# A third token tile's attention in halves, and a later gate, in an adaptive-layernorm transformer block

## What is computed

```python
mod = (silu(c) @ wmod).reshape(4, 6, 1, -1)            # c (4, 1024), wmod (1024, 6144)
sa, ca, ga, sb, cb, gb = (mod[:, i] for i in range(6))
ga, gb = (2 * (g >= 0) - 1) * max(abs(g), 0.25)        # for g = ga and g = gb
h = layernorm(x) * (1 + ca) + sa                       # x (4, 512, 1024)
x = x + ga * (h @ (weight * block_mask).T)             # "attention": 1024 x 1024, mask of 32 x 32 blocks
h = layernorm(x) * (1 + cb) + sb
x = x + gb * ffn(h)                                    # NF4 codes, hidden size 2752, silu(h w1) * (h w2) @ w3
```

## Time and profile before

| | |
|---|---|
| median of 3 runs | 1569.68 us (1569.42 to 1570.12) |
| the profiled execution's own time | 1569.33 us |
| its span, first to last instruction | 1567.6 us |
| outside the span | 1.7 us |
| PE busy in the span | 1539.4 us, 98% |
| DVE busy | 1029.5 us, 66% |
| ACT busy | 989.6 us, 63% |

### The profile page before, as it was taken

The page is one execution under the profiler, slowest core; times in us unless marked ns, Lnnn a source line. Parts: engine busy times, 40 slices in busy tenths (PEclk is TensorE's granted clock), DMA queues, the critical chain, the costliest instruction groups (busy, mean ns, idle before and its releaser), DMA issues.

```text
span 1567.6 us, 19154 instructions
## 1 busy us (share of the span) xinstructions
PE 1539.4 (98%) x7200; PEld 1269.6 (81%) x7200; DVE 1029.5 (66%) x1486; ACT 989.6 (63%) x1290; POOL 5.5 (0%) x10
## 2 busy tenths in 40 slices
PE   5899999999999999999999999999999999999999
PEld 3688888888888888888888888888888888888887
DVE  5687786555555455547676666666875757956994
ACT  3475676998888888884898988785433432333220
POOL 0000000000000000000000000000000000000000
PEclk9999999999999999999999999999999999999999
DMA  9976423564555445532778787786777868947973
GB/s 368 372 258 228 134 81 138 177 200 166 186 169 187 153 162 180 178 128 97 257 228 252 207 250 208 207 254 171 260 292 272 332 204 302 343 160 268 397 279 122
DMA packets 170139, 345.97 MB, mean 221 GB/s; under 512 B 14752, under 2 KB 65344, under 8 KB 170048
## 3 DMA queue, kind: packets, MB, share of 16 engines
q1 hardware_dynamic: 170048, 344.76, 65.1%
HBM read 249.77 MB, written 94.93 MB: 220 GB/s over the span
## 4 chain that ended last, share of the span: by engine, by line
PE 96%; DMA 2%; DVE 0%; ACT 0%; SPq 0%; issue 0%
PE ps L1916 10%; PE ps L1915 10%; PE ps L1914 10%; PE ps L1988 9%; PE ps L1987 9%; PE ps L1989 9%; PE ps L1925 9%; PE ps L1927 9%; PE ps L1926 9%; PE ps L1832 4%; PE ps L1834 4%; PE ps L1833 4%; DMA wmod<-wmod 2%; PE ps L1789 2%; PE ps L1772 1%; DVE attn_w_lo L1368 0%
## 5 line engine op out<-in xcount | busy, mean ns | idle before, releaser
L861 ACT ACTIVATE w_raw<-w_raw 128x1024 f32<-128x1024 f32 x287 | 304.6, 1061 | 9.1
L1914 PE MATMUL ps<-ffn_in_hi,w_hi 128*128 128x512 f32 x688 | 268.6, 390 | 0.0
L1916 PE MATMUL ps<-ffn_in_hi,w_lo 128*128 128x512 f32 x688 | 267.8, 389 | 0.0
L1915 PE MATMUL ps<-ffn_in_lo,w_hi 128*128 128x512 f32 x688 | 267.7, 389 | 0.0
L1987 PE MATMUL ps<-t_hi,s_hi 128*128 128x512 f32 x616 | 239.6, 389 | 0.0
L1988 PE MATMUL ps<-t_lo,s_hi 128*128 128x512 f32 x616 | 239.6, 389 | 0.0
L1989 PE MATMUL ps<-t_hi,s_lo 128*128 128x512 f32 x616 | 239.6, 389 | 0.0
L1925 PE MATMUL ps<-x_m_hi,stream_hi 128*128 128x512 f32 x604 | 235.0, 389 | 0.0
L1926 PE MATMUL ps<-x_m_lo,stream_hi 128*128 128x512 f32 x604 | 235.0, 389 | 0.0
L1927 PE MATMUL ps<-x_m_hi,stream_lo 128*128 128x512 f32 x604 | 235.0, 389 | 0.0
L1114 ACT ACTIVATE s_hi<-s_raw 128x1408 fp32r<-128x1408 f32 x56 | 77.4, 1383 | 241.2 <-DVE s_raw L1624 192.6
(11 more groups left out here) (136 smaller groups left out, 2078.1 us busy)
## 6 DMA issues: line engine op xcount, KB each, us to landing
s_raw<-h_d SPq DMA_DIRECT2D x96, 704.0 KB, 5.6
stream_raw<-t_d SPq DMA_DIRECT2D x150, 256.0 KB, 3.4
t_d<-combined SPq DMA_DIRECT2D x106, 256.0 KB, 2.6
wmod<-wmod SPq DMA_DIRECT2D x12, 2048.0 KB, 15.3
t_raw<-w_d SPq DMA_DIRECT2D x88, 256.0 KB, 6.1
w_codes<-w12q SPq DMA_DIRECT2D x41, 512.0 KB, 5.3
h_d<-h_tile SPq DMA_DIRECT2D x44, 256.0 KB, 2.4
h_d<-up_c SPq DMA_DIRECT2D x44, 256.0 KB, 3.3
```

Of the source, the lines that this page charges most:

```text
L861: act.activation(RAWF[r], RAWF[r] if j else RQ[r][:], ACT.Prelu, bias=bias, scale=sign, alpha=slope).then_inc(line_ready, 1)
L1914: pe.matmul(acc, RH[r][:, k, :], HH[:, b, k, :], start=(k == 0), stop=False)
L1915: pe.matmul(acc, RH[r][:, k, :], HL[:, b, k, :], start=False, stop=False)
L1916: last = pe.matmul(acc, RL[r][:, k, :], HH[:, b, k, :], start=False, stop=(k == C - 1))
```

## The change

Tile 2 is treated like tiles 0 and 1: its modulation and attention are done by halves of d, in PSUM banks 6 and 7, and its operands lie in two new tiles over a weight piece (80 and 84 KB). The transpose banks stay 4 and 5; group 1's wmod product moves to bank 4, group 2's (the gate) to bank 0, behind tile 0's `set_aside`; groups 3 to 5 stay in bank 6, now behind tile 2's residual. x of tile 2 is loaded ahead of mask pieces 2 and 3, which get places of their own. Parts 4 and 5 (the gate) are multiplied after all of tile 2's attention and after `turn1(3)`. Parts 6 and 7 move from behind tile 2 to behind tile 4, parts 8 and 9 from behind tile 5 to behind tile 6, their loads to t = 2 of SP's loop; group 3's rows are copied at t = 5 and turned after tile 5. On DVE `ln1(3)`, `ln1(4)`, `low_part1(3)` and `ln1(5)` come ahead of the gate, and `low_part1(4)` behind it, ahead of tile 0's residual. On ACT `input1(4)` comes ahead of `root(1, 0)`.

```diff
-    MOD_BANK, TURN_BANK, MASK_BANK = (0, 6, 6, 6, 6, 6), {0: 3, 1: 7, 3: 6, 4: 6}, 7
+    MOD_BANK, TURN_BANK, MASK_BANK = (0, 4, 0, 6, 6, 6), {0: 3, 1: 4, 3: 6, 4: 6}, 7
+    BY_HALVES = 3
+    HALF_TURNS = [(0, 0), (1, 0), (0, 1), (0, 2), (1, 1), (1, 2)]
...
@@ SP @@
             load_weight(0)
+            load_x(2)
             load_mask(2)
...
             load_weight(3)
-            sp.wait_ge(mask_step, MASK_STEPS + 2)
-            load_x(2)
             load_x(3)
...
             load_ga(TPB)
-            load_wmod(8)
...
-                if t == 1:
+                if t == 2:
+                    load_wmod(8)
                     load_wmod(9)
@@ ACT @@
             weight_high(0)
+            root(0, 2)
             act.wait_ge(mod_read, 2)
             half_input1(0, 0)
             half_input1(0, 1)
+            norm1(2)
+            half_input1(0, 2)
             weight_high(2)
...
             half_input1(1, 1)
+            start1(3)
+            half_input1(1, 2)
+            start1(4)
+            input1(3)
+            start1(5)
+            input1(4)
+            root(1, 0)
+            for t in range(2, TILES):
...
-                if t in (2, 6):
-                    copy_rows(t // 4 + 3)
+                if t in (5, 7):
+                    copy_rows(t // 2 + 1)
@@ DVE @@
             read_mod(0)
+            ln1_sums(2)
             split_weight(0)
             half_low_part1(0, 0)
+            ln1_factors(2)
             sum_mask(2)
...
             mask_weight(2)
+            half_low_part1(0, 2)
             split_weight(2)
...
-            ln1(2)
             ln1(3)
             set_aside(0)
-            low_part1(2)
+            half_low_part1(1, 2)
+            ln1(4)
             set_aside(1)
+            low_part1(3)
+            ln1(5)
             gate(0)
-            ln1(4)
-            ln1(5)
-            low_part1(3)
+            low_part1(4)
             residual_sum(0)
             residual_norm(0)
             for t in range(2, TILES):
                 residual_sum(t - 1)
-                if t == 2:
-                    low_part1(4)
-                elif t == 4:
+                if t == 4:
                     low_part1(5)
...
-                if t in (5, 8):
-                    read_mod(t // 3 + 2)
+                if t in (6, 8):
+                    read_mod(t // 2)
@@ PE @@
-                    if m == 2:
-                        pe.wait_ge(rows_read, 2)
+                    if m == 1:
+                        pe.wait_ge(half_modulated1, half_at(0, 2))
+                    elif m == 2:
+                        pe.wait_ge(gated, 1)
                     elif m == 3:
-                        pe.wait_ge(gate_step, 2)
+                        pe.wait_ge(gated, 3)
...
             attend_first(1, 0, 0)
+            half_turn1(0, 2)
             sum_partitions(1)
             modulation(2)
+            attend_first(2, 0, 0)
             modulation(3)
             attend_first(0, 1, 0)
             turn_mod(1, 1)
             attend_first(1, 1, 0)
             half_turn1(1, 1)
+            attend_first(2, 1, 0)
             attend_first(0, 0, 1)
             attend_first(0, 1, 1)
+            half_turn1(1, 2)
             attend_first(1, 0, 1)
-            turn1(2)
             attend_first(1, 1, 1)
+            turn1(3)
+            attend_first(2, 0, 1)
+            attend_first(2, 1, 1)
             modulation(4)
             modulation(5)
-            for t in range(2, TILES):
+            for t in range(BY_HALVES, TILES):
...
-                if t in (4, 7):
-                    turn_mod(t // 3 + 2, t // 3 + 1)
-                for j in {2: (6, 7), 5: (8, 9), 8: (10, 11)}.get(t, ()):
+                if t in (5, 7):
+                    turn_mod(t // 2 + 1, t // 2)
+                for j in {4: (6, 7), 6: (8, 9), 8: (10, 11)}.get(t, ()):
                     modulation(j)
```

More of the change, by code:

```diff
@@ L93, in adaln_kernel @@
     WM = [at(f"wmod_{i}", [C // 2, D], F32, kb) for i, kb in enumerate((0, 16, 64))]
-    MP = [at(f"mask_piece_{i}", [C // 2, HALF], I32, kb) for i, kb in enumerate((96, 104, ST + 8, ST + 28))]
+    MP = [at(f"mask_piece_{i}", [C // 2, HALF], I32, kb) for i, kb in enumerate((96, 104, 112, 120))]
     WP = [at(f"weight_piece_{i}", [C // 2, HALF], F32, kb) for i, kb in enumerate((80, 88, 128, 144))]
@@ L102, in adaln_kernel @@
     AL = [at(f"attn_in_lo_{i}", [C, P], F32R, 152 + 4 * i) for i in range(2)]
+    A3 = [at(f"attn_in_third_{n}", [C, P], F32R, kb) for n, kb in (("hi", 80), ("lo", 84))]
     raw_kb = (168, 172, 160, 164)
@@ L277, in adaln_kernel, with half_turns, half_at, attn_bank @@
     out_made = sem("out_made")
-    MOD_BANK, TURN_BANK, MASK_BANK = (0, 6, 6, 6, 6, 6), {0: 3, 1: 7, 3: 6, 4: 6}, 7
+    MOD_BANK, TURN_BANK, MASK_BANK = (0, 4, 0, 6, 6, 6), {0: 3, 1: 4, 3: 6, 4: 6}, 7
+    TURN_FROM = {0: 0, 1: QUARTER, 3: 0, 4: 0}
+    BY_HALVES = 3
+    HALF_TURNS = [(0, 0), (1, 0), (0, 1), (0, 2), (1, 1), (1, 2)]
+    def half_turns(half, t):
+        return HALF_TURNS.index((half, t)) + 1
+    def half_at(half, t):
+        return BY_HALVES * half + t + 1
+    def attn_bank(t):
+        return 6 if t == 2 else 2 * (t % 2)
+    def hi_of(t):
+        return A3[0] if t == 2 else AH[t % 2]
+    def lo_of(t):
+        return A3[1] if t == 2 else AL[t % 2]
     LN_STEPS, GATE_STEPS = 9, 5
@@ L295, in whole @@
     def whole(t):
-        return t - 1
+        return t - BY_HALVES + 1
     def place2(e):
@@ L911, in half_input1 @@
             def half_input1(half, t):
-                e = 2 * half + t
                 cs = slice(HALF_C * half, HALF_C * (half + 1))
-                act.wait_ge(half_turned, 2 * t + half + 1)
+                act.wait_ge(half_turned, half_turns(half, t))
                 if t:
-                    act.wait_ge(half_low1, e)
+                    act.wait_ge(half_low1, half_at(half, t) - 1)
                 for c in range(HALF_C * half, HALF_C * (half + 1)):
@@ L921, in half_input1 @@
                 ins.then_inc(half_modulated1, 1)
-                act.wait_ge(half_modulated1, e + 1)
-                act.activation(AH[t][:, cs, :], HM[0][:, cs, :], ACT.Copy).then_inc(half_high1, 1)
+                act.wait_ge(half_modulated1, half_at(half, t))
+                if t == 2:
+                    act.wait_ge(w_lo, weight_at(0))
+                act.activation(hi_of(t)[:, cs, :], HM[0][:, cs, :], ACT.Copy).then_inc(half_high1, 1)
             def input1(t):
                 act.wait_ge(turned1, whole(t))
-                if t >= 3:
+                if t > BY_HALVES:
                     act.wait_ge(low1, whole(t - 1))
                 else:
-                    act.wait_ge(half_low1, 4)
+                    act.wait_ge(half_low1, 2 * BY_HALVES)
                 modulate(4, HM[0], MODS[0], batch_of(t), modulated1, whole(t))
-                act.wait_ge(attn_done, t - 1)
+                act.wait_ge(attn_done, 1 if t == 4 else t - 1)
                 act.activation(AH[t % 2][:], HM[0][:], ACT.Copy).then_inc(high1, 1)
@@ L988, in _ @@
             half_input1(1, 1)
[L989 to L1007, removed]
+            start1(3)
[6 more added lines that the diff above has]
+            for t in range(2, TILES):
+                both = t - 2 >= HALF_TILES
+                if both:
+                    input2(t - 2 - HALF_TILES)
+                elif t > 4 and t + 1 < TILES:
+                    input1(t + 1)
+                root(1, t - 1)
+                if both and t + 1 < TILES:
+                    input1(t + 1)
                 if t == 3:
@@ L1276, in half_low_part1 @@
                 cs = slice(HALF_C * half, HALF_C * (half + 1))
-                dve.wait_ge(half_high1, 2 * half + t + 1)
-                dve.tensor_tensor(AL[t][:, cs, :], HM[0][:, cs, :], AH[t][:, cs, :].bitcast(F32), ALU.subtract).then_inc(half_low1, 1)
+                dve.wait_ge(half_high1, half_at(half, t))
+                dve.tensor_tensor(lo_of(t)[:, cs, :], HM[0][:, cs, :], hi_of(t)[:, cs, :].bitcast(F32), ALU.subtract).then_inc(half_low1, 1)
             def low_part1(t):
@@ L1839, in attend_half @@
                     pe.wait_ge(low1, whole(t))
-                    pe.wait_ge(gated, t - 1)
+                    if t == 4:
+                        pe.wait_ge(gate_step, 1)
+                    else:
+                        pe.wait_ge(gated, t - 1)
                 last = attend_part(t, hb, range(C))
@@ L1846, in attend_first @@
                 pe.wait_ge(w_lo, weight_at(2 * hb + half))
-                pe.wait_ge(half_low1, 2 * half + t + 1)
+                pe.wait_ge(half_low1, half_at(half, t))
                 last = attend_part(t, hb, range(HALF_C * half, HALF_C * (half + 1)))
```

28 lines of the change are left out of this document (14 added, 14 removed).

## The result

| | before | after |
|---|---|---|
| median of 5 runs | 1569.47 us | 1586.03 us (1585.74 to 1586.85) |
| ratio | | 1.0104 (1.009 to 1.0117) |
| profiled execution: time, span | 1569.33, 1567.6 us | 1585.9, 1583.9 us |

The change made the kernel slower by 16.6 us; the forecast was +16.4, between 1574 and 1590.

The account below looks back on a forecast made before the run. PE, fully busy from 84.6 us, was taken to bound the kernel, so only delays to PE count. The profiled 1569.33 plus 14.8 (late `turn1(7)` and parts 8, 9) plus 1.6 (clock) gave 1585.7 us, range 1574 to 1590.

Parts of the forecast that it names:

- The start: Up to part 5: tile 2's halves fill PE's early gaps; part 5 ends at 80.2, PE 4.4 us ahead.
- the lead: PE's gain on the old order at the end of part 5: 4.4 us, +-1 from DVE's split.
- The gate's move: Gate behind parts 4 and 5 lands at 90.3; tile 2's residual 3.7 us late; PE waits 5.9 us for `norm1(6)`.
- The loads in a row: Parts 8 and 9 issued together delay tile 3's x2 store; tile 7's x lands at 130.7, DVE waits 9 us.
- The rows' place: ACT copies group 3's rows only behind `norm1(7)`, until 138.8; PE waits from 128, `turn1(7)` starts at 139.75.
- The clock: Lower clock behind PE's 10 us gap ahead of group 3's turn: +1.6 us (0 to 3.4).
- the first term: At `turn1(7)`: 11.2 us late, with parts 8 and 9 (3.6 us) still ahead, summing to +14.8 us.
- the store's landing: Tile 3's x2 store, issued at 113.0 behind parts 8 and 9, lands at 126.4 (bounds 116.3 and 127).
- the gain is gone: At tile 6's turn: PE's 4.4 us lead is lost to a 5.9 us wait; tile 5's attention starts near 115.9.

Follow-up runs that it names:

- b_gate: The kernel before, with only the load of the attention gate for tile 0 held until tile 2's attention is done: 1573.39 us, ratio 1.0021.
- a_xslot: The changed kernel, with x of tile 7 in a place of its own, loaded behind the gate: 1576.16 us, ratio 1.0034.
- b_loads: The kernel before, with only the loads of wmod parts 8 and 9 moved, both to t = 2 of SP's loop: 1581.8 us, ratio 1.0069.
- b_loads_xslot: The kernel before, with wmod parts 8 and 9 both loaded at t = 2 and x of tile 7 in its own place: 1569.85 us, ratio 1.0001.
- a_rows: The changed kernel, with ACT copying group 3's rows at t = 4 instead of t = 5: 1583.64 us, ratio 1.0085.
- a_warm: The changed kernel, with 48 identity matmuls put into PE's wait ahead of group 3's turn: 1586.83 us, ratio 1.0102.
- after_again: The changed kernel unedited, run again for comparison on the same chip: 1586.52 us, ratio 1.0104.
- a_g7: The changed kernel, with tile 7's x in its own place and wmod part 7 loaded behind the gate's loads: 1574.36 us, ratio 1.0027.
- a_best2: The changed kernel, with early x loads in own places, DVE and ACT work moved into waits, and parts 10 and 11 loaded later: 1567.26 us, ratio 0.9984.

## Why the prediction was right

Time, range and sign came out as forecast (1585.7 against 1586.0), and so did the mechanism, step by step. That the time was met to 0.3 us is in part luck, since errors of opposite sign cancel in it (below):

- **The start.** The gap ahead of part 2 was 1.55 us (1.4), and the clock did not fall behind it (1.00 from 41.3 to 43.3). Part 3 at full clock (1.00): 46.16 to 48.1, 1.93 us (forecast 1.9 to 2.0). DVE's split of piece 1 beside POOL took 4.31 us (forecast 4.4):

```profile
52.91 4.31 DVE L1389 TENSOR_TENSOR attn_w_lo<-weight_piece,attn_w_hi 128x2048 fp32r<-128x2048 f32 x1 [0.61 <-ACT attn_w_hi L994]
...
57.74 2.28 DVE L1389 TENSOR_TENSOR attn_w_lo<-weight_piece,attn_w_hi 128x2048 fp32r<-128x2048 f32 x1
```

  The same work without POOL beside it takes 2.28 us. POOL's own operation ran from 51.42 to 55.07, so 2.16 us lie under both, and the split is 2.03 us longer, nearly as much as the overlap. In the kernel before the same operation took 3.57 us against 2.29 without POOL, 1.28 us longer for 1.42 us under both. The two amounts go together in both traces; no view shows how POOL's operation holds DVE's up. Part 5 ended at 79.5, not 80.2: the lead was 5.1 us, not 4.4. It made no difference, since the lead was lost at the next long wait.
- **The gate's move.** Issued at 85.96 (86.2), landed and used at 90.08 (90.3); tile 2's residual at 102.23 (102.2); `norm1(6)` done at 112.13 + 1.23 = 113.36 (113.5); PE's wait 6.15 us (5.9), tile 5's attention at 115.92 (115.9). b_gate shows that a late gate costs time by itself, and a_xslot, with x of tile 7 out of the way, is still 5.8 us above the kernel before.
- **The loads in a row.** The normalized store ahead of the parts was issued at 109.70 (109.7), the parts at 110.06, the store of x2 at 113.00 (113.0), x of tile 7 at 125.75 (126.5), so the store took 12.7 us where it took 3.3 before; x landed at 130.06 (130.7), DVE waited 8.48 us (9). b_loads has the same in the kernel before, 124.28 - 109.89 = 14.4 us, and with x in a place of its own (b_loads_xslot, a_xslot) it no longer costs anything. The store and the parts are on one queue, and the store behind them landed after 12.7 and 14.4 us against 3.3; in what order the queue's transfers are worked off no view shows.
- **The rows' place.** Rows copied from 136.57 to 138.09 (138.8), PE's wait to 138.14. a_rows confirms that this place is worth little by itself, 3.0 us of 16.
- **The clock.** `turn1(7)` at 139.11 instead of 139.75, which makes the first term 139.11 - 128.57 + 3.6 = 14.1 us and not 14.8; with tile 8's turn 16.2 us late, 2.0 us are left for the clock and not 1.6. One error hid the other. The 1.6 was an estimate from part 3, which took 3.62 us behind a wait of 3.20 where 1.9 was counted at full clock, and was put on a wait three times as long; that a price carries over from one wait to another no run shows, and the runs had 1.5 to 3.9 us (the last section). The clock fell while PE stood:

```profile
107.50:113.30 5.80, 0.00 (x0) 0.00 (x0) 5.37 (x17) 5.12 (x11) 0.00 (x0) 0.66 0.49 148
113.40:119.40 6.00, 5.45 (x16) 4.37 (x17) 5.75 (x13) 4.54 (x6) 0.00 (x0) 0.50 1.00 390
138.10:143.40 5.30, 5.26 (x22) 4.71 (x23) 4.04 (x11) 3.22 (x8) 0.00 (x0) 0.50 0.46 188
```

  It is 0.50 when PE comes back, and stays there for 6.0 us behind the first wait and 5.3 behind the second. a_warm puts the price of the second at 1.6 us (beside after_again). The first costs 2.8: from the turn of tile 6 to the end of tile 5's attention PE takes 128.81 - 113.41 - 0.55 = 14.85 us, before 124.98 - 112.97 = 12.0. The prediction gave it about 1 us; here that is hidden under the second wait, in a_xslot it is not.

**What was off.** The terms of the sum were each off by less than a microsecond: the lead by 0.7, the store's landing by 0.7, `norm1(7)` by 0.6. The store's landing was also added up wrongly: rows 11 and 12 give 113.0 + 12.3 = 125.3, or 126.0 counted from the parts, and not 126.4; measured 125.7. That "the gain is gone" rests on one fact I used but did not weigh: behind 85 us the other engines had less slack than the lead of 5.1 us. In the kernel before DVE's product of tile 2 ends 1.2 us ahead of tile 4's attention, `norm1(6)` (109.81) 3.2 us ahead of its turn, `norm1(7)` (124.57) 4.0 us. My expectations of the first two experiments were worse than the prediction. For b_loads I put a stall of 4.5 us at the turn and measured +11.4 in all, because DVE's read of group 3 stands behind tile 7's layernorm and PE wants it ahead of part 8, which I had followed in the changed kernel only as far as the rows' copy. For b_gate I looked for the stall at tile 5 and it was at tile 4, by a PSUM bank.

**What stays open.** How much of a_xslot's remaining 5.8 us is the gate and how much `ln1(6)` behind it was not separated: the gate came 3.7 us late, but with it in time `norm1(6)` would still have ended near 109.8 (an estimate, its time before), 2.5 us behind PE's coming at 107.3. Whether the store would wait behind the parts on another queue too was not run. That part 7 ahead of the gate's loads costs anything is not settled by a_g7's time.

## What to carry to other kernels

Full PE says nothing of how closely the other engines follow it: before an early gap is filled, take the slack of each engine, in its own order of work, behind it. Where this was less than the lead, here 3.2 us against 5.1 at tile 6's turn, the lead was lost at the first wait, and the restart at the lower clock (0.50) cost extra, 2.8 us and 2.0. The moved loads were paid for by what stood next in their queue, a 0.5 MB store behind 4 MB that took 12.7 us instead of 3.3, and by the load that waits for that store's slot; give that load a slot of its own, or put the big ones behind it. A wait names the last in line (here ACT's copy of the rows): take the cause away, not only the last step.

## What the runs showed of the hardware

- The clock fell behind a short wait: in b_gate PE stood for 2.36 us and the 3 us behind it ran at 0.50.

```profile
103.00:106.00 3.00, 2.96 (x7) 2.41 (x8) 2.89 (x7) 1.97 (x3) 0.00 (x0) 0.50 0.98 299
```

  Waits of 1.08 us, 1.55 us (ahead of part 2) and 2.08 us (a_best2) had no low clock behind them: 1.00 from 57.0 to 58.5, from 41.3 to 43.3 and from 110 to 113.
- What the lower clock cost did not follow the length of the wait in these runs. Behind 2.36, 3.20 and 8.91 us (b_gate, the kernel before, b_loads) it cost 1.5 to 1.7 us, behind 9.33 us (the changed kernel) 2.0. The wait of 6.15 us ahead of tile 6's turn was the dearest: 2.8 us in the changed kernel and, with the same wait, 3.9 in a_xslot, where PE worked for 8.4 us at 0.50:

```profile
113.80:122.20 8.40, 7.85 (x22) 6.21 (x23) 8.04 (x19) 6.97 (x13) 0.00 (x0) 0.50 1.02 390
```

  So a price taken from one gap was off here by a factor of two (1.7 and 3.9 us).
- SP waited 2.7 us for four stores of 4 KB with part 7's 2 MB ahead of them (the changed kernel), and 1.0 us with part 7 behind them (a_g7).
